# A fused per-patch block on one core: a shorter group of small VectorE operations, the squares as one ScalarE operation, two of three bias-and-relu steps on ScalarE, and a new order on every engine

## The reference, cut to what matters

```python
x_norm = jnp.sqrt((patches ** 2).sum(axis=1))
y = einsum('ncij,vc->nvij', patches, w_mask) / (x_norm * w_norm)   # both centred by a layer norm before
idx = argmax(y.reshape(NL, -1), axis=1); max_sim = the value there
max_act, vc_vec = the patch's best pixel, the best prototype
integrate = max_act * max_sim + vc_vec * (1.0 - max_sim)
h = leaky_relu(concat([integrate, sim_map_max]) @ w_i1.T + b_i1, 0.2)
vcs = tanh(h @ w_i2.T + b_i2)
h2 = relu(vcs @ w_l1.T + b_l1) @ w_l2.T + b_l2
t = patches + conv(h2)                      # the residual
out = t + ffn(layernorm_over_channels(t))   # 96 -> 384 -> 96, products of 8-bit, sums of 16-bit floats
```

## Time and profile before

| | us |
|---|---|
| median of 3 runs (2236.76 to 2238.84) | 2237.98 |
| the profiled execution | 2232.82 |
| its span, first to last instruction | 2231.0 |
| DVE busy | 2111.6 (95%) |
| PE busy | 2007.8 (90%) |
| ACT busy | 1834.2 (82%) |
| POOL busy | 1548.6 (69%) |

### The profile page before, as it was taken

The page is one execution under the profiler, slowest core; times in us unless marked ns, Lnnn a source line. Parts: engine busy times, 40 slices in busy tenths (PEclk is TensorE's granted clock), DMA queues, the critical chain, the costliest instruction groups (busy, mean ns, idle before and its releaser), DMA issues.

```text
span 2231.0 us, 47761 instructions
## 1 busy us (share of the span) xinstructions
PE 2007.8 (90%) x13105; PEld 1485.3 (67%) x13105; DVE 2111.6 (95%) x7422; ACT 1834.2 (82%) x5381; POOL 1548.6 (69%) x1041
## 2 busy tenths in 40 slices
PE   5889999999999999999999999999999999999865
PEld 4566766667666676666766667676666766767653
DVE  7889999999999999999999999999999999999952
ACT  1158888888888888888888888888888888888886
POOL 2467677777767767677676777767777677777742
PEclk9899999999999999999999999999999999999975
DMA  3212323222232232322323232232322323223101
GB/s 98 76 58 81 99 82 107 81 91 96 87 101 82 90 97 85 103 81 91 97 84 104 82 97 92 89 98 82 105 83 89 99 81 99 89 89 98 42 37 48
DMA packets 65481, 193.34 MB, mean 87 GB/s; under 512 B 13688, under 2 KB 15938, under 8 KB 65218
## 3 DMA queue, kind: packets, MB, share of 16 engines
q1 hardware_dynamic: 52866, 170.80, 23.8%
q0 software_dynamic: 10240, 18.89, 2.9%
q10 hardware_dynamic: 2112, 0.60, 0.1%
HBM read 133.23 MB, written 57.02 MB: 85 GB/s over the span
## 4 chain that ended last, share of the span: by engine, by line
DVE 42%; PE 23%; POOL 22%; issue 11%; ACT 2%; POOLq 1%; DMA 0%; ACTq 0%; DVEq 0%
DVE best_y L1031 14%; POOL xl L400 6%; DVE stats L1040 5%; PE bank L701 5%; POOL prod L379 5%; POOL o_pm L391 4%; POOL t_dev L368 4%; DVE h L1048 4%; PE y_ps L646 3%; POOL tq L356 3%; PE y_ps L648 3%; PE y_ps L647 3%; DVE top_v L1070 2%; DVE w_index L1077 2%; DVE t_pm L1056 2%
## 5 line engine op out<-in xcount | busy, mean ns | idle before, releaser
L1031 DVE TENSOR_REDUCE best_y<-y_ps 128x2 f32<-128x1024 f32 (+1 forms) x640 | 698.0, 1107 | 17.5 <-PE y_ps L648 14.6
L463 ACT CAST y<-bank 128x384 f16<-128x384 f32 x1152 | 554.1, 481 | 72.8 <-PE bank L671 68.4
L646 PE MATMUL y_ps<-proto_hi,xh 96*128 96x512 f32 x1152 | 573.4, 498 | 43.6 <-DVE best_y L1031 16.1
L356 POOL TENSOR_TENSOR tq<-t_dev,ra 128x864 fp8e5<-128x864 f32 x128 | 209.4, 1636 | 537.8 <-DVE ra L1012 537.8
L671 PE MATMUL bank<-tqt,f_w 96*128 96x384 f16 x1152 | 392.6, 341 | 141.6 <-ACT y L463 110.4
L472 ACT ACTIVATE h<-h 128x1152 fp8e5<-128x1152 f16 x384 | 448.8, 1169 | 68.3 <-DVE h L1048 68.2
L647 PE MATMUL y_ps<-proto_lo,xh 96*128 96x512 f32 x1152 | 460.4, 400 | 0.0
L648 PE MATMUL y_ps<-proto_hi,xl 96*128 96x512 f32 x1152 | 459.6, 399 | 0.0
L671 PEld LDWEIGHTS bank<-tqt,f_w 96*128 96x128 f16 x1152 | 111.6, 97 | 382.2 <-ACT y L463 266.6
L400 POOL TENSOR_TENSOR xl<-xc,xh 96x1152 fp32r<-96x1152 f32 x128 | 336.9, 2632 | 26.5 <-ACT xh L533 15.8
L1048 DVE TENSOR_SCALAR h<-y,f_b 128x1152 f16<-128x1152 f16 x384 | 306.9, 801 | 22.5 <-ACT y L463 22.5
(11 more groups left out here) (133 smaller groups left out, 4115.9 us busy)
## 6 DMA issues: line engine op xcount, KB each, us to landing
xc<-x_cm SPq DMA_DIRECT2D x128, 432.0 KB, 3.9
xp<-x_pm SPq DMA_DIRECT2D x128, 432.0 KB, 4.6
out<-o_pm SPq DMA_DIRECT2D x128, 432.0 KB, 2.4
xsel<-x_pm,x_index POOLq DMA_INDIRECT x128, 2.5
wsel<-proto_rows,w_index POOLq DMA_INDIRECT x128, 4.7
proto_rows<-proto SPq DMA_DIRECT2D x1, 384.0 KB, 2.7
proto<-w_mask SPq DMA_DIRECT2D x1, 192.0 KB, 3.7
f_f<-w_1t ACTq DMA_DIRECT2D x1, 144.0 KB
```

The lines of the kernel that those rows point to most:

```text
L463: act.copy(y16[:, q, r, 0:TOK], bank[0][:, 0:TOK]).then_inc(s_y16, 1)
L646: pe.matmul(y, hi, proto_hi[:], start=True, stop=False)
L1031: dve.tensor_reduce(best_y[t % 2][:, j0:j1], y_ps[n % 2][:, 0:j1 - j0, :], AX_X, ALU.max).then_inc(s_yd, 1)
```

## The change

On VectorE the short group loses operations: the product with the norm and its maximum are one operation with a running maximum; the row bases come from a table and are not added up; two sums are one of 18 numbers; one operation makes both kinds of variances; the inverse square root takes 7 steps for 9, on 36 numbers for 27 (a better first guess and a polynomial of fourth degree). The squares of t are one ScalarE operation of 864 numbers, summed by a new VectorE operation, `t_squares`. The bias and relu of the thirds 0 and 1 of the hidden layer move to ScalarE (`hidden16`); third 2 stays. All four engines' orders are new.

```diff
+            def hidden16(s, stage, q):
+                if run.live(s, stage):
+                    t = s - stage
+                    run.wait(s_y16, NC * t + 3 * (q + 1))
+                    run.wait(s_h8, NH * (t - 1) + q + 1)
+                    act.activation(h16[:, q, :, 0:P].rearrange("p (r j) l -> p r j l", r=3),
+                                   y16[:, q, :, 0:TOK].rearrange("p r (j l) -> p r j l", l=P), ACT.Relu,
+                                   bias=f1_b[:, q:q + 1]).then_inc(s_h16[q], 1)
...
-            def squares(s, js):
...
-                        ins = act.activation(sq_junk[:, j * C:(j + 1) * C], t_dev[t % 2][:, j * C:(j + 1) * C],
-                                             ACT.Square, accum_out=sq_t[:, j:j + 1])
+            def squares(s):
...
+                    act.activation(t_sq[:], t_dev[t % 2][:], ACT.Square).then_inc(s_sq, 1)
...
             def slot(s):
+                high(s)
                 ffn1_out(s, 0)
-                high(s)
                 vcs_out(s)
+                weighted(s)
                 ffn1_out(s, 1)
                 hidden8(s, FFN2, 1)
                 ffn1_out(s, 2)
                 xnt_out(s)
-                mix_out(s)
+                hidden16(s, FFN, 0)
                 layer1_out(s)
...
             def slot(s):
+                gather_x(s)
                 lock(s)
                 t_norm(s)
-                gather_x(s)
+                product(s)
+                low_h(s)
+                low_x(s)
                 t_center(s)
-                product(s)
                 output(s)
-                low_x(s)
-                low_h(s)
                 gather_w(s)
...
-                    steps.done("cos", dve.tensor_tensor(cosj[:], best_y[t % 2][:], ra[t % RING][:, 0:J], ALU.mult))
+                    steps.done("top", dve.tensor_tensor_reduce(cosj[:], best_y[t % 2][:], ra[t % RING][:, 0:J], 1.0, -3e38,
+                                                               ALU.mult, ALU.max, top[t % 4][:, 0:1]))
...
+            def t_squares(s):
+                if run.live(s, NORM):
+                    run.wait(s_sq, s - NORM + 1)
+                    ins = dve.tensor_reduce(va[s % 2][:, J:2 * J], t_sq[:].rearrange("p (j c) -> p j c", c=C), AX_X, ALU.add)
+                    ins.then_inc(s_sqd, 1)
```

More of the change, by code:

```diff
@@ L214, in build @@
         s_y16 = sem("y16_ready")
-        s_h16 = sem("h16_ready")
+        s_h16 = [sem(f"h16_ready{q}") for q in range(NH)]
         s_h8 = sem("h8_ready")
@@ L258, in done, with need @@
                 self.kept[name] = self.n
-            def need(self, name):
-                self.run.wait(s_dve, self.kept[name])
+            def need(self, *names):
+                self.run.wait(s_dve, max(self.kept[name] for name in names))
         N_SETUP = 22
         POOL_A = 5
-        POOL0 = 13
+        POOL0 = 14
         N_DVE0 = 13
@@ L327, in _ @@
                 step(pool.memset(tq[b][:], 0.0))
-            step(pool.memset(va[:], 1.0))
+            for b in range(2):
+                step(pool.memset(va[b][:], 1.0))
             step(pool.memset(vcs[C:C + 1, :], 1.0))
@@ L468, in hidden8 @@
                     t = s - stage
-                    run.wait(s_h16, NH * t + q + 1)
+                    run.wait(s_h16[q], t + 1)
                     run.wait(s_f2, 2 * (t - 1))
@@ L588, in slot @@
                 ffn1_out(s, 8)
-                squares(s, range(7, 9))
+                hidden8(s, FFN, 0)
             run.slots(slot)
@@ L867, in _ @@
             step(dve.tensor_copy(iota_j[:], iota_i[:, 0:J]))
-            step(dve.tensor_copy(row_base[:], iota_i[:, J:J + 1]))
+            step(dve.tensor_copy(row_base[:], iota_i[:, J:]))
+            step(dve.memset(eps[:, 0:J], 1e-6))
+            step(dve.memset(eps[:, J:], 1e-5))
+            for b in range(4):
+                step(dve.memset(top[b][:], 3e38))
             steps = Steps(run, once[0])
@@ L913, in pick_root @@
                     t = s - SELECT
+                    steps.need("one")
                     steps.done("sel", dve.tensor_tensor_reduce(
-                        junk_rstd[:], one_j[:], ra[t % RING][:, J:2 * J], 1.0, 0.0, ALU.mult, ALU.add, sel_rstd[t % 2][:]))
-            def next_rows(s):
-                if run.live(s, SELECT):
-                    steps.done("rows", dve.tensor_scalar(row_base[:], row_base[:], float(JP), None, ALU.add))
+                        junk_rstd[:], one_j[:], ra[t % RING][:, 2 * J:3 * J], 1.0, 0.0, ALU.mult, ALU.add, sel_rstd[t % 2][:]))
             def low_part(s):
@@ L931, in x_dif, with x_sum @@
                     steps.done("dif", dve.tensor_tensor(m_dif[:], st[:, :, 1], st[:, :, 4], ALU.subtract))
-            def x_two(s):
-                if run.live(s, MATCH):
-                    st = stats[(s - MATCH) % 2]
-                    steps.done("two", dve.tensor_tensor(m_two[:], st[:, :, 2], st[:, :, 5], ALU.add))
-            def x_mean(s):
+            def x_sum(s):
                 if run.live(s, MATCH):
@@ L941, in x_mean @@
                     st = stats[t % 2]
-                    steps.done("mean", dve.tensor_tensor(mean2_x[t % RING][:], st[:, :, 1], st[:, :, 4], ALU.add))
+                    steps.need("x")
+                    steps.done("sum", dve.tensor_tensor(x_sums[t % RING][:], st[:, :, 1:3], st[:, :, 4:6], ALU.add))
             def x_sq(s):
@@ new lines, in root @@
+                    if k == 3:
+                        steps.need("w")
+                        steps.done("first", dve.scalar_tensor_tensor(r_u[:], r_v[:], QUARTIC[0], r_v[:], ALU.add, ALU.mult))
+                    if k == 4:
+                        steps.done("second", dve.scalar_tensor_tensor(r1[:], r_v[:], QUARTIC[2], r_v[:], ALU.add, ALU.mult))
+                    if k == 5:
+                        steps.need("first")
+                        steps.done("part", dve.scalar_tensor_tensor(r_t[:], r_u[:], QUARTIC[1], r_t[:], ALU.add, ALU.mult))
@@ L1025, in y_max @@
+                    if k == 6:
+                        steps.need("part")
+                        dve.scalar_tensor_tensor(r[:], r1[:], QUARTIC[3], r_t[:], ALU.add, ALU.mult).then_inc(s_rt, 1)
             def y_max(s, g):
```

210 lines of the change are left out of this document (91 added, 119 removed).

## The result

The changed kernel takes 2304.4 us in the median of four runs (2300.19 to 2314.79), the kernel before 2238.4 beside it: a ratio of 1.030 with a 95% interval of 1.027 to 1.034. It is slower by 3%, where the prediction said faster by 4%, and the time lies above its range. The profiled execution took 2302.92 us, its span is 2301.1. Two executions among all that follow, one of the kernel before (2521.1 us) and one of experiment 5 (3863.4 us), fell into a slower state and are in no ratio; without it experiment 5 has 2421.4 us.

What follows compares the result with a forecast made beforehand. VectorE bound the old kernel; a ring through the gather would bound the new at 15.6 us a slot for 16.36. Over 121 slots that saves 92 us, less 4 at the end: 2145, plus 5.2 to the median, 2150 us (2085 to 2215).

Steps and rivals of the forecast that it cites:

- the short group: VectorE's run of small operations: 27 instructions for 32, 2.9 us (2.6 to 3.3), saving 0.75 us a slot.
- The ring: Loop from gather issue through ScalarE's early `weighted`, TensorE and VectorE to the next gather: 15.6 us, bounding the slot.
- The landing: Gather's issue to the row's landing, with store and both loads starting beside it: 4.7 us, ends 2.6 and 6.3.
- The handover to the gather: GpSimd's 0.16 us ahead of the gather, counted within about 0.35 us for four handovers.
- Rival 2: Slower, gather lands late: over 5.45 us a slot passes 16.36; at 6.3 it is 17.2, 2344 us; chance 0.09.
- The new VectorE work: VectorE's own work in a slot falls from 16.36 to 15.1 us.
- The squares as one operation: On ScalarE, one square of 864 numbers replaces nine: 0.8 us by width, 1.07 at most.
- Rival 1: No closed loop, engines bound the slot: landing 2.6 to 4.0 us, 2077 to 2114 us, say 2110; chance 0.34.
- Rival 3: Engines do not pack: a further 0.4 to 0.7 us a slot, 2190 to 2233 us; chance 0.08.
- Rival 4: VectorE's group not shorter and ScalarE's new operations take 1.8 us: nothing left, 2238 us; chance 0.04.

Runs made afterwards that it cites:

- experiment 5: Kernel before the change with only `weighted` moved early in ScalarE's slot, behind `vcs_out`: 2422.5 us, ratio 1.082 to the kernel before.
- experiment 1: Changed kernel with `weighted` back at its old late place, behind the copy of bank 0 numbered 5: 2072.6 us, ratio 0.926 to the kernel before.
- experiment 2: Changed kernel with SyncE issuing the store one slot later, behind the next two loads, `weighted` still early: 2084.1 us, ratio 0.932 to the kernel before.
- experiment 6: Changed kernel with five added TensorE passes of 512 columns ahead of `ffn1` 2, where TensorE waits: 2290.3 us, ratio 1.022 to the kernel before.
- experiment 7: Kernel of experiment 1 with bias and relu of thirds 0 and 1 back on VectorE: 2216.6 us, ratio 0.992 to the kernel before the change.
- experiment 12: Kernel of experiment 1 with `gather_w` ahead of `output` on GpSimd: 2248.8 us, ratio 1.0055 to the kernel before the change.
- experiment 3: Changed kernel with both `weighted` back at its late place and the store issued one slot later: 2071.5 us, ratio 0.926 to the kernel before.
- experiment 8: Kernel of experiment 1 with squares as nine ScalarE operations with their own sums, no sum on VectorE: 2307.7 us, ratio 1.032 to the kernel before.

## Why the prediction was wrong

**The mechanism was right, its length was not.** The ring was named, and experiments 1 and 2 open it from two sides (232 and 220 us). Its parts, those between `wterm` and the next gather from a slot with a full clock (1118.21 to 1133.48, above), the rest over the 95 slots:

| part | predicted | measured |
|---|---|---|
| gather to `wterm` | 4.7 | 3.8 to 5.9, mean 5.1 |
| ScalarE, `wterm` to the copy's end | 2.2 | 2.2 |
| TensorE, to the third reduction | 3.3 | 3.4 |
| VectorE, to the end of the index search | 5.05 | 5.07 |
| handovers | 0.35 | 0.85 |
| loss by the halved clock | 0 | 0.5, mean |
| slot | 15.6 | 17.16 |

*The landing.* The step "4.7 or more is nearer than 2.6; I take 4.7" failed. The argument ahead of it was right: store and loads start with the gather. But it took the value of a gather with the two loads alone as the value with a store added, and a median over all gathers where the middle of the run had already 4.9 in the mean of the 95. With store, loads and gather within a microsecond it is 5.5 in the mean, to the start of `wterm` (63 of the 95 slots of the changed kernel), and 5.1 in the median of experiment 1; 2 to 3 us behind the store it is 4.3 (21 slots). The prediction worked out from the Trainium skill's rule that a transfer engine takes its queues in turn ("DMA: Bandwidth & Descriptors", "SWDGE vs HWDGE vs iDMA") that a longer queue would add nothing and 4.7 would stay; the traces don't agree with that, the row came 0.4 to 0.6 us later. +0.4 a slot.

*The handover to the gather.* Taken as 0.16 from the earlier trace rows, where the index had been there for microseconds. A gather that truly waits for it starts 0.8 us behind the search's end (1117.39 to 1118.21, 1132.66 to 1133.48); in 85 of the 95 slots the gather waited so, each time 0.81 to 0.83 us. +0.5.

*The clock.* Left out of the sum. The expected 0.3 us and more of waiting became 2.0 us on ScalarE (1.9 on TensorE in the slot shown), and behind 32 of the 95, most of them the longer ones, the clock was at the lower level, in the slot shown for 6.4 us, in passes that lie on the ring. +0.5 in the mean. The share of the clock can't be read as a gain to be had: experiment 6 gave it back, and of the kernel's time only 14 us went.

The first two alone make a slot of 16.5 (16.6 by the measured parts) and pass the old 16.4, so the sign was wrong without the clock. Rival 2 was this mechanism. Its threshold of 5.45 us held for a rest of 10.9; with the true rest of 11.5 it is 4.9, and the mean landing of the kernel before was already 4.9 over the 95 slots. Given 0.09, it was underpriced because one term's uncertainty was counted and the other terms were taken as exact. That its 2344 us is nearer to the 2304 measured is in part luck: it took a landing of 6.3, and the rest came from the handover and the clock.

**Right.** The new VectorE work: 15.0 us measured, 15.1 predicted. The short group, from its first step to zb less `t_squares` (both in the changed kernel, 1117.89 to 1121.69):

```profile
1117.89 0.16 DVE L970 TENSOR_TENSOR mix_in<-simraw,ra 128x9 f32<-128x9 f32 x1
...
1118.62 1.03 DVE L1048 TENSOR_REDUCE va<-t_sq 128x9 f32<-128x864 f32 x1
1119.59 0.15 DVE L953 TENSOR_TENSOR va<-x_sums,m_sq 128x9 f32<-128x9 f32 x1
...
1121.69 0.60 DVE L998 TENSOR_TENSOR zb<-z,f_b 128x864 f16<-128x864 f16 x1
```

3.80 - 0.97 = 2.83 us (predicted 2.9). The squares as one operation: 0.81 to the next start (0.8). `hidden16` cost more than the rows gave:

```profile
L476 ACT ACTIVATE h<-y,f_b 128x1152 f16<-128x1152 f16 x256 | 321.6, 1256 | 1.1 <-issue 0.3
L487 ACT ACTIVATE h<-h 128x1152 fp8e5<-128x1152 f16 x384 | 452.4, 1179 | 0.0
```

1,256 ns against 1,179 for the same width without a bias per partition: +77, a pitch of 1.16 (1124.30 to 1125.46 on ScalarE) for the 1.07 taken. The Trainium skill's 93 ns ("ScalarE: Activation LUTs", "What ACT_TABLE_LOAD costs") came closer than the nearest row. Its rule that gives relu to VectorE (same page, "Rules for kernel authors") did not hold here: experiment 7 shows 144 us of gain from the opposite, since VectorE was the bound.

**Rival 1** is what the change is worth without the ring: 15.0 to 15.3 us a slot. Experiment 1 has 15.2 and 2072.6 us, just below its 2077 to 2114, since the ramp gained too (29 us up to the sixteenth gather). **Rival 3** fell: at 97% busy on three engines the order packs. Its own terms (0.4 to 0.7 us a slot on 2150) give 2198 to 2235 and not the 2190 to 2233 written, which changes nothing. **Rival 4** fell with the 2.83 us of the short group.

## What to carry to other kernels

When an instruction that waits for a small transfer is moved early on an engine, write out the ring from the transfer's issue back to it, and price every term with a row in which that term really waits: a handover read where the data had long been there is too short, and a landing read with less traffic beside it is a lower bound. If the ring comes within a microsecond of the engines' own work, leave the wait late: here 232 of 2304 us hung on one line. A transfer that nobody waits for may land 2.4 us later at no cost (5.1 in experiment 1 for 2.7 in experiment 12). Hurrying it by a new order on GpSimd cost 168 and 176 us here; moving the store on SyncE cost nothing, and was needed only where the wait stood early.

## What was not expected of the hardware

- The row of a small gather lands after 2.7 us when nothing starts with it (experiment 12), 3.1 with a store (experiments 2 and 3), 4.7 with two loads before the change, 5.1 with store and loads (experiment 1), medians over 128 gathers, 64 in experiment 2.
- A gather that waits for an index from VectorE starts 0.82 us behind the end of the search.
- Behind a wait of 1.90 us TensorE's passes ran at the lower clock for 6.4 us, pitch 0.43 for 0.23, and this made a way of 11.49 us 13.67.
- A VectorE addition of nine numbers with two operands in SBUF was held until a GpSimd step over 864 numbers ended: 1.3 us in the mean for 0.15. Operations with one SBUF operand beside GpSimd's steps were not.
- Open: the clock's dips in experiment 8, and a split of the loss between late rows and clock that would hold under a change, since they feed each other.
